# Attention passes of a graph kernel: 64 of 231 edge groups as one-hot matmuls on TensorE, the rest gathered

## The chip, the cores and the metric

One NeuronCore of one Trainium2 chip. The time is the device time of one execution of the whole program, in microseconds; the median of three runs before the change is 11624.68 us (11606.98 to 11636.15).

## What is computed

A graph of 6250 nodes with 64 features and 206250 edges, sorted by destination, goes through eight message-passing layers: three SAGE layers, two weighted GIN layers and three GAT (attention) layers, with residual additions and layer norms between and at the end. The change is about the attention layers, and about the first SAGE pass, which prepares lists for later ones. An attention layer, with 8 heads of 8 features:

```python
h = (x @ W.T).reshape(N, H, C)
alpha_s = jnp.einsum('nhc,hc->nh', h, a_src)
alpha_d = jnp.einsum('nhc,hc->nh', h, a_dst)
e = _leaky_relu(alpha_s[src] + alpha_d[dst])
e_max = jax.ops.segment_max(e, dst, num_segments=N)
e_exp = jnp.exp(e - e_max[dst])
denom = jax.ops.segment_sum(e_exp, dst, num_segments=N)
alpha = e_exp / denom[dst]
msg = alpha[:, :, None] * h[src]
out = jax.ops.segment_sum(msg, dst, num_segments=N)
```

## The kernel before

**Groups.** The edges stand in 231 groups (NG) of 7 x 128 (G columns on P partitions). As they are sorted, the destinations of a group lie in a window of WIN = 32 nodes. Sums and maxima of the destinations are kept transposed in SBUF, features on partitions and nodes along the row: accT (72 rows: 64 sums and 8 denominators), xT (running maxima of the source scores, rows 0 to 7), auxT (rows 0 to 7: alpha of the destination).

**An attention pass** (gat_pass, three times) has five engines in order, each with a body(n) that works on several groups at different stages; the loops are unrolled. GpSimd gathers for each group 7 x 128 rows of 72 numbers from gat_table in DRAM by seven indirect DMAs (L2285), into a ring of GR = 12 buffers. ScalarE (L2380 to L2410) does in body n: factors(n-3), weights(n-5), over_lowest(n), which is the source score minus the lowest (L2399). VectorE in body n: exponents(n-4), shifts(n-2), columns_in_quads(n-3), over_layers(n-1), chosen(n), in_layers(n), turned_choice(n), messages(n-5), add_sums(n-7). TensorE: sums(n-6), values(n-3), shifts(n-2), turn_maxima(n-1), layer_maxima(n). The maximum over the edges of a destination is found by laying the scores in ten layers (LAYERS), so that edges of one destination are in different ones, multiplying with the one-hot of the destination, and a maximum over layers. If a new group raises a destination's maximum, the sums so far are multiplied by a factor. The semaphores that matter below: VectorE's exponents(g) waits for p_ready of weights(g-1) (its buffer z is single); TensorE's values(g) waits for avm_ready of VectorE's columns_in_quads(g), which needs TensorE's shifts(g) of a body earlier; TensorE's layer_maxima(n) waits for VectorE's in_layers(n). SyncE loads each group's destinations.

```python
for n in range(NG + 6):
    body(n)
```

**Cells.** The sage and gin passes don't gather most of their rows. Four groups (GB) make a block, 46 blocks in all, and the edges of a block are scattered by GpSimd (scatter, L1001) into 52 cells (TS), by the source modulo 52, in up to SL = 112 slots. Source s is row s // 52 of cell s % 52 of the node table, which lies in SBUF as X[partition, cell, feature], so that a one-hot of the source's partition (near) times the cell's nodes, split in three bf16 parts, gives the rows (fetch, L1049), and a one-hot of the destination (far_hot, fp32) times the messages gives the sums (add_cells, L1069). A block is worked in 13 pieces (NPC) of 4 cells (PC). The first sage pass makes these lists: slots come from a rank, the number of earlier edges in the same cell (rank_event on TensorE, L1109; earlier_in_bins, place on VectorE), over all 28 columns of the block at once. It stores the near one-hots (near_keep, SyncE, near_table) for all blocks, and for blocks with even number the product of both one-hots (adjacency L1059, keep L1385) and for odd ones the destination and weight of each slot (note, L1393). A check (overflow) sends all passes to a general way where a cell is too full.

The attention pass needs a score and a maximum for each edge, and before the change uses no cells.

## Time and profile before

| | |
|---|---|
| median of 3 runs | 11624.68 us |
| profiled execution | 11634.58 us, span 11632.5 us |
| TensorE busy | 8371.0 us (72%), mean granted clock 0.677 of 2.4 GHz |
| VectorE busy | 7236.0 us (62%) |
| ScalarE busy | 2833.5 us (24%) |
| GpSimd busy | 8097.8 us (70%) |
| DMA | 1285.98 MB, mean 111 GB/s |

Engines: PE is TensorE (PEld its weight loads), DVE VectorE, ACT ScalarE, POOL GpSimd, SP SyncE. The first sage pass runs to about 2430 us, two further sage passes to about 3800, two gin passes to about 4950, and the attention passes from 5140 to the end at 11632.

The page cuts the span in 40 slices and gives busy tenths, the granted clock in tenths of 2.4 GHz, and DMA:

```profile
PE   4878888889999799956666667566666666666665
PEld 3777777768778687835555555455555545555553
DVE  5777777779999654565555556555555565555556
ACT  2444333434444455520000001100000020000001
POOL 5777777737577475727777775677777757777774
PEclk9898888979999898955555555555555555555555
```

A fp32 matmul shows as two MATMUL and two LDWEIGHTS instructions. Shapes read partitions x elements; for TensorE rows x columns of the weights and then of the moving operand.

### The profile page before, as it was taken

The numbers are of one execution on the slowest core, as the hardware profiler recorded it, in microseconds if no ns is written. First come the engines' busy times: TensorE is split into PE (matmuls) and PEld (weight loads), VectorE is DVE, ScalarE is ACT, GpSimd is POOL, SyncE is SP. The second block draws the span as 40 slices with busy tenths as digits, with TensorE's granted clock in tenths as the row PEclk, the third lists the DMA queues.
The fourth block names the chain that finished last, engine by engine and source line by source line (L and its number), as shares of the span: only waits on it lengthen the run. The fifth ranks groups of instructions, "written<-read, shape, count | busy, mean of one in ns | idle before, by whom it ended". The sixth has DMA issues, their size and how long they took to land. (4 is left out here: it accounts for less than half of the span.)

```text
span 11632.5 us, 269882 instructions
## 1 busy us (share of the span) xinstructions
PE 8371.0 (72%) x95122; PEld 6886.6 (59%) x95123; DVE 7236.0 (62%) x21427; ACT 2833.5 (24%) x9590; POOL 8097.8 (70%) x8039
## 2 busy tenths in 40 slices
PE   4878888889999799956666667566666666666665
PEld 3777777768778687835555555455555545555553
DVE  5777777779999654565555556555555565555556
ACT  2444333434444455520000001100000020000001
POOL 5777777737577475727777775677777757777774
PEclk9898888979999898955555555555555555555555
DMA  4666666649899686812222221222222212222221
GB/s 133 189 188 190 188 178 182 187 127 258 222 257 258 193 267 210 254 25 43 43 43 43 43 43 33 43 43 43 43 43 43 43 33 43 43 43 43 43 43 28
DMA packets 1192998, 1285.98 MB, mean 111 GB/s; under 512 B 234298, under 2 KB 1039893, under 8 KB 1191410
## 3 DMA queue, kind: packets, MB, share of 16 engines
q1 hardware_dynamic: 629602, 628.36, 17.7%
q0 software_dynamic: 254464, 283.59, 12.8%
q10 hardware_dynamic: 307600, 356.66, 10.6%
q8 instruction: 788, 12.91, 0.5%
q14 instruction: 544, 4.46, 0.1%
HBM read 982.93 MB, written 284.81 MB: 109 GB/s over the span
## 5 line engine op out<-in xcount | busy, mean ns | idle before, releaser
L2285 POOL DMA_INDIRECT rows<-gat_table,wgt x2457 | 2353.5, 958 | 962.2 <-issue 747.9
L2285 POOL DMA_INDIRECT Y<-gat_table,wgt x2394 | 2293.6, 958 | 729.6 <-issue 729.6
L2466 DVE TENSOR_TENSOR rep<-rep,layers 128x560 f32<-128x560 f32 x693 | 514.9, 743 | 2372.6 <-ACT rep L2399 2372.6
L1001 POOL DMA_INDIRECT bins<-scratch,slots x1288 | 1373.2, 1066 | 500.0 <-issue 384.9
L2311 PE MATMUL bank<-rep,work 128*32 128x80 f32 x11088 | 527.7, 341 | 1495.5 <-DVE rep L2466 1495.5
L2311 PEld LDWEIGHTS bank<-rep,work 128*32 128x32 f32 x11088 | 324.0, 158 | 1836.6 <-DVE rep L2466 1836.6
L2358 PE MATMUL bank<-work,msg 128*72 128x32 f32 x9702 | 1308.7, 309 | 0.0
L2358 PEld LDWEIGHTS bank<-work,msg 128*72 128x72 f32 x9702 | 1215.8, 237 | 44.5
L1191 DVE TENSOR_TENSOR xT<-counts,xT 112x480 f32<-112x480 f32 x1716 | 1114.5, 650 | 80.0 <-issue 48.3
L1069 PE MATMUL bank<-xT 112*64 112x120 f32 (+1 forms) x13728 | 1138.5, 277 | 26.4 <-ACT xT L1379 24.4
L2345 PE MATMUL bank<-scratch,work 128*128 128x64 f32 x2772 | 754.8, 426 | 515.5 <-DVE scratch L2436 515.5
L1012 POOL DMA_INDIRECT rows<-node_table,listed x826 | 916.6, 1110 | 266.1 <-issue 251.0
L1069 PEld LDWEIGHTS bank<-xT 112*64 112x64 f32 (+1 forms) x13728 | 1025.3, 142 | 87.8 <-ACT xT L1379 46.4
L1379 ACT ACTIVATE xT<-xT 112x256 f32<-112x256 f32 x1716 | 712.0, 415 | 1433.7 <-DVE xT L1196 1228.0
L2345 PEld LDWEIGHTS bank<-scratch,work 128*128 128x128 f32 x2772 | 643.5, 323 | 609.5 <-DVE scratch L2436 609.5
L1196 DVE TENSOR_TENSOR xT<-scores,xT 112x256 f32<-112x256 f32 x1344 | 562.7, 419 | 476.0 <-PE scores L1049 431.5
L1569 POOL DMA_INDIRECT rows<-node_table,listed x658 | 698.6, 1062 | 202.0 <-issue 200.1
L2399 ACT ACTIVATE rep<-rows,rep 128x56 f32<-128x56 f32 x351 | 119.8, 341 | 2812.4 <-DMA rows<-gat_table,wgt 2812.4
L2399 ACT ACTIVATE rep<-Y,rep 128x56 f32<-128x56 f32 x342 | 116.7, 341 | 2722.3 <-DMA Y<-gat_table,wgt 2722.3
L1049 PE MATMUL scores<-work 128*128 128x64 bf16 x11344 | 648.5, 195 | 47.8 <-DMA work<-near_table 35.9
L1654 DVE TENSOR_TENSOR scratch<-counts,scratch 112x480 f32<-112x480 f32 x598 | 393.8, 659 | 402.1 <-PE scores L1605 394.3
L1049 PEld LDWEIGHTS scores<-work 128*128 128x128 bf16 x11344 | 525.8, 99 | 87.1 <-DMA work<-near_table 45.4
(277 smaller groups left out, 16940.1 us busy)
## 6 DMA issues: line engine op xcount, KB each, us to landing
xT<-bins ACTq DMA_DIRECT2D x1716, 119.0 KB
work<-adj SPq DMA_DIRECT2D x184, 780.0 KB
work<-near_table SPq DMA_DIRECT2D x1118, 128.0 KB
near_table<-work SPq DMA_DIRECT2D x598, 128.0 KB
xT<-near_table SPq DMA_DIRECT2D x598, 128.0 KB
adj<-work ACTq DMA_DIRECT2D x299, 240.0 KB
bins<-zeros ACTq DMA_DIRECT2D x46, 1547.0 KB, 9.6
work<-in_attr SPq DMA_DIRECT2D x231, 224.0 KB
```

The costliest lines, as they stand in the source:

```text
L1001: nc.gpsimd.indirect_dma_start(bins, bass.IndirectOffsetOnAxis(slots[b % RANK_LEAD][:, r * G + j:r * G + j + 1], 0), binf[r][:, j, :], Non ...
L1012: nc.gpsimd.indirect_dma_start(rows[s][:, k, 0:D], None, table, bass.IndirectOffsetOnAxis(listed_of(n + g0, k), 0)).then_inc(s_rows[s].han ...
L1049: last = nc.tensor.matmul(joint[k % JR][0:SLW, c * D:(c + 1) * D], found[:, c * SLW:(c + 1) * SLW], part_of[:, i * PC + c, :], start=n == ...
L1069: last = nc.tensor.matmul(half_sums(u, c % HALVES), cellf[k % RR][0:SL, c, 0:width], far_hot[k % RR][0:SL, c * MW:(c + 1) * MW], start=i = ...
L1191: nc.vector.tensor_tensor(far_hot[s][0:SL, :].rearrange("p (c m) -> p c m", m=MW), bc(counts[0:SL, 1:MW + 1], [SL, PC, MW], 1), bc(payf[s] ...
L1196: nc.vector.tensor_tensor(cellf[s][0:SL, :, 0:D], joint[k % JR][0:SL, 0:PC * D].rearrange("p (c d) -> p c d", d=D), payf[s][0:SL, :, 0:D], ...
L1379: nc.scalar.activation(cellf[s][0:SL, :, 0:D], cellf[s][0:SL, :, 0:D], ACT.Relu).then_inc(q["cells_ready"].handle, 1)
L1569: nc.gpsimd.indirect_dma_start(rows[s][:, k, 0:D], None, table, bass.IndirectOffsetOnAxis(listed_of(n + g0, k), 0)).then_inc(s_rows[s].han ...
L2285: nc.gpsimd.indirect_dma_start(rows[g % GR][:, j, :], None, gat_table, bass.IndirectOffsetOnAxis(edge_sources[:, g * G + j:g * G + j + 1], ...
L2311: last = nc.tensor.matmul(dense[c * WIN:(c + 1) * WIN, k // QUAD * LH:(k // QUAD + 1) * LH], sels[g % SR][:, j, :], layered[:, j * LH:(j + ...
L2345: last = nc.tensor.matmul(edge[:, h * QUAD * 2 * H:(h * QUAD + n) * 2 * H], choice[g % RR][0:n * WIN, h * P:(h + 1) * P], avm4[0:n * WIN, ...
L2358: last = nc.tensor.matmul(wide[g % 2][0:ROW, 0:WIN], msg[g % R][:, j, :], sels[g % SR][:, j, :], start=j == 0, stop=j == G - 1)
```

## The change

In each attention pass, the four groups of 16 odd-numbered blocks (1, 3, ..., 31), 64 groups, are not gathered. They are worked as blocks of cells; the other 167 groups go as before, over a list `order`.

- The first sage pass stores two more tables for these 16 blocks: far_table, the fp32 one-hots of the destination (far_keep, on SyncE), and far_turned, their transposes in bf16. These are made on TensorE (turn_far: the destination numbers spread over the partitions, in the bank of adjacency) and on ScalarE (keep_turned: the square of the difference, then relu(1 - square), two ACTIVATEs and a store per piece).
- The rank now counts group by group, so that within a cell the edges are in order of destination. That takes 70 matmuls instead of 28 for each block (rank_event).
- A new block `repeats` reads the notes of the 16 blocks and compares slots 8 apart (CELL_LAYERS); if any two have the same destination, all passes go the general way.
- alpha of the destination moves from auxT to accT rows 96 to 103 (ALPHA), and auxT holds gat_table in three bf16 parts, which each pass makes at its start from 13 chunks (table_load, table_high, table_rest, table_middle, table_low). In shifts the copy of alpha comes first and is waited for.
- The ring of gathered rows has 8 buffers (GR) instead of 12.
- The cell work of a block is laid out in 35 steps, a new block every 19 (LAG), in all 320, over the 174 bodies of a pass; half of a body's steps stand before TensorE's layer_maxima and VectorE's chosen, the others at the end; on ScalarE they all stand at the end of the body. In steps 0 to 12 a piece is fetched (cell_fetch), taken by ScalarE (cell_take) and laid in eight layers, and one step later multiplied with the destination one-hots (cell_layer), then reduced (cell_reduce). Step 14 turns the maxima (cell_turn), 15 does the shifts of 120 destinations (cell_shift, cell_column), 16 and 17 carry the destinations' values to the slots by the turned one-hots (cell_value), 17 and 18 the exponents and weights, 18 to 30 the messages, 19 to 31 the sums (cell_sum), 32 to 34 the output is turned and added.

Both one-hots and tables are loaded by SyncE, in rings of 6 (near and turned, 131 KB each) and 4 (far, 215 KB each).

```diff
-GR = 12
+GR = 8
+CELL_LAYERS = 8
+CELL_BLOCKS = 16
+LAG = 19
+LAST = 35
...
-                        for j in range(GT):
-                            last = nc.tensor.matmul(rank_sum, earlier16[:], hot[:, j, :], start=j == 0, stop=j == GT - 1)
+                        for r in range(GB):
+                            of_group = rank_sum[:, r * TS:(r + 1) * TS]
+                            for j in range((r + 1) * G):
+                                last = nc.tensor.matmul(of_group, (earlier16 if j >= r * G else ones16)[:], hot[:, j, :],
+                                                        start=j == 0, stop=j == (r + 1) * G - 1)
...
+                    def keep_turned(b, i):
...
+                        nc.scalar.activation(apart_of, adj_sum[:, 0:PC * SL], ACT.Square, bias=minus_part1[:]).then_inc(q["far_apart"].handle, 1)
...
+            order = [g for g in range(NG) if not (g < GB * NBK and g // GB % 2 == 1 and g // GB // 2 < CELL_BLOCKS)]
+            GN, DELAY = len(order), 7
+            bodies = GN + DELAY
...
+            all_steps = LAG * (CELL_BLOCKS - 1) + LAST
...
+            MAXED, COLUMNS, VALUES, WEIGHED, SUMMED, OUT = NPC + 1, NPC + 2, NPC + 3, NPC + 5, NPC + 6, 2 * NPC + 6
+
+            def active(s):
+
+                return [(k, s - LAG * k) for k in range(CELL_BLOCKS) if 0 <= s - LAG * k < LAST]
+
+            def steps_of(n):
+
+                at = [(n + i) * all_steps // (bodies - 2) for i in [-1, 0]]
+                steps = list(range(max(at[0], 0), min(max(at[1], 0), all_steps)))
+                return steps[:(len(steps) + 1) // 2], steps[(len(steps) + 1) // 2:]
...
+                    def cell_fetch(k, i):
+                        hots = hot_of("near", k, i)
+                        wait(pe, (q["cells_ready"], piece(k, i)), (q["low_ready"], NCH))
+                        for c in range(PC):
+                            for n, part_of in enumerate(table_parts):
+                                last = nc.tensor.matmul(found_bank[0:SLW, c * ROW:(c + 1) * ROW], hots[:, c * SLW:(c + 1) * SLW], part_of[:, i * PC + c, :],
+                                                        start=n == 0, stop=n == 2)
+                        last.then_inc(q["fetched"].handle, 1)
+
+                    def cell_layer(k, i):
+                        fars = far_of("layer", k, i)
+                        wait(pe, (q["cells_ready"], piece(k, i) + 1), (q["layers_reduced"], piece(k, i)))
+                        for c in range(PC):
+                            last = nc.tensor.matmul(layer_bank[0:MW, c * CL:(c + 1) * CL], fars[:, c * MW:(c + 1) * MW], cell_layered[piece(k, i) % 2][0:SL, c * CL:(c + 1) * CL],
+                                                    start=True, stop=True)
+                        last.then_inc(q["cells_layered"].handle, 1)
...
+                    def cell_value(k, h):
+                        wait(pe, (q["column_parts_ready"], k + 1), (q["cell_z_ready"], 2 * k + h))
...
+                    def cell_sum(k, i):
...
+                        for c in range(PC):
+                            last = nc.tensor.matmul(cell_sums[0:MW, 0:ROW], fars[:, c * MW:(c + 1) * MW], cell_msg[piece(k, i) % 2][0:SL, c, :],
+                                                    start=i == 0 and c == 0, stop=i == NPC - 1 and c == PC - 1)
...
                     def body(n):
                         if real(n - 6):
                             sums(n - 6)
...
                         if real(n - 1):
                             turn_maxima(n - 1)
+                        for s in steps_of(n)[0]:
+                            cell_step(s)
                         if real(n):
                             layer_maxima(n)
+                        for s in steps_of(n)[1]:
+                            cell_step(s)
...
+                    def cell_take(k, i):
+                        x = piece(k, i)
+                        wait(ac, (q["fetched"], x + 1), (q["cell_msg_ready"], x - NPC + 1), (q["cells_layered"], x - 1))
+                        found_of = found_bank[0:SL, 0:PC * ROW].rearrange("p (c w) -> p c w", w=ROW)
+                        layers_of = cell_layered[x % 2][0:SL, :].rearrange("p (c l h) -> p c l h", l=CELL_LAYERS, h=H)
+                        nc.scalar.activation(cell_rows[0:SL, i * PC:(i + 1) * PC, :], found_of[:, :, 0:D], ACT.Copy)
+                        nc.scalar.activation(cell_above[0:SL, i * PC:(i + 1) * PC, :], found_of[:, :, D:ROW], ACT.Identity, bias=minus_lowest[0:SL, :])
+                        for n in range(CELL_LAYERS):
+                            last = nc.scalar.activation(layers_of[:, :, n, :], found_of[:, :, D:ROW], ACT.Identity,
+                                                        bias=lowest_layers[0:SL, n:n + 1], scale=cell_layers[0:SL, n:n + 1])
+                        last.then_inc(q["cells_ready"].handle, 1)
...
                         if real(n):
                             over_lowest(n)
-
-                    for n in range(NG + 5):
+                        for s in [*steps_of(n)[0], *steps_of(n)[1]]:
+                            cell_step(s)
+
+                    for n in range(bodies):
                         body(n)
...
+                    def cell_reduce(k, i):
+                        wait(ve, (q["cells_layered"], piece(k, i) + 1))
+                        nc.vector.tensor_reduce(cell_maxima[0:MW, i * H:(i + 1) * H], layer_bank[0:MW, 0:PC * CL].rearrange("p (x h) -> p h x", h=H), AX, ALU.max
+                                                ).then_inc(q["layers_reduced"].handle, 1)
...
                         if real(n - 1):
                             over_layers(n - 1)
+                        for s in steps_of(n)[0]:
+                            cell_step(s)
                         if real(n):
                             chosen(n)
                             in_layers(n)
...
                         if real(n - DELAY):
                             add_sums(n - DELAY)
+                        for s in steps_of(n)[1]:
+                            cell_step(s)
```

## Rows read from the trace of the kernel before

**Rows 1.** Windows: us, busy (x instructions) PE PEld DVE ACT POOL, clock, DMA share, GB/s.

```profile
500.00:1500.00 1000.00, 811.76 (x9910) 732.22 (x9908) 749.64 (x1519) 403.93 (x1243) 781.99 (x716) 0.89 0.65 190
5250.00:6750.00 1500.00, 944.55 (x7139) 762.20 (x7138) 780.10 (x3227) 144.56 (x680) 1137.62 (x1190) 0.50 0.22 43
```

**Rows 2.** Page, costliest groups: L2285, busy, mean ns | idle before, releasers.

```profile
L2285 POOL DMA_INDIRECT rows<-gat_table,wgt x2457 | 2353.5, 958 | 962.2 <-issue 747.9
L2285 POOL DMA_INDIRECT Y<-gat_table,wgt x2394 | 2293.6, 958 | 729.6 <-issue 729.6
```

**Rows 3.** Lines L2285 and L2521 in the first attention pass: min/median/max ns, first, last.

```profile
L2285 POOL DMA_INDIRECT rows<-gat_table,wgt x819: 940/944/1508, 5139.9 to 7178.4; - x164
...
L2521 DVE TENSOR_TENSOR accT<-accT,bank x231: 182/183/186, 5214.2 to 7205.8; 72x32 f32 x116
```

**Rows 4.** Waits, 5300 to 6900 us: us in total, times, longest.

```profile
ACT rep L2399 <- DMA Y<-gat_table,wgt: 723.2, 91, 8.9
```

**Rows 5.** Groups of GpSimd, 500 to 1500 us, columns as in rows 2.

```profile
L1001 POOL DMA_INDIRECT bins<-scratch,slots x570 | 616.2, 1081 | 173.8 <-issue 173.2 <-ACT scratch L1403 0.6
L1012 POOL DMA_INDIRECT rows<-in_x,listed x146 | 166.8, 1143 | 44.5 <-issue 44.5
```

**Rows 6.** Timeline, second sage pass: start, us, engine, line, operation, idle before it.

```profile
3304.16 0.52 PE L1049 MATMUL scores<-work 128*128 128x64 bf16 x12
...
3304.72 0.42 DVE L1196 TENSOR_TENSOR xT<-scores,xT 112x256 f32<-112x256 f32 x1 [0.16 <-PE scores L1049]
```

**Rows 7.** Timeline, one body of the first attention pass.

```profile
7003.87 0.21 ACT L2384 ACTIVATE Y<-dif 8x32 f32<-8x32 f32 x1
7003.99 0.74 DVE L2466 TENSOR_TENSOR rep<-rep,layers 128x560 f32<-128x560 f32 x1 [3.34 <-ACT rep L2399]
...
7004.25 0.25 ACT L2392 ACTIVATE msg<-zpos 128x56 f32<-128x56 f32 x1
...
7004.79 0.76 PE L2311 MATMUL bank<-rep,work 128*32 128x80 f32 x16 [2.05 <-DVE rep L2466]
...
7005.83 0.21 DVE L2449 TENSOR_TENSOR z<-rows,bank 128x56 f32<-128x56 f32 x1
...
7006.18 0.94 POOL L2285 DMA_INDIRECT Y<-gat_table,wgt  x1 [0.30 <-issue]
...
7007.15 0.18 DVE L2502 TENSOR_TENSOR U<-xT,auxT 8x32 f32 x1 [0.60 <-issue]
...
7008.82 0.30 DVE L2475 TENSOR_REDUCE rep<-bank 128x8 f32<-128x160 f32 x1
7008.94 0.93 PEld L2345 LDWEIGHTS bank<-scratch,work 128*128 128x128 f32 x4 [0.84 <-DVE scratch L2436]
...
7010.91 0.60 PE L2324 MATMUL bank<-ident,rep 128*8 128x128 f32 x2
```

**Rows 8.** Timeline of ScalarE, second gin pass.

```profile
4555.90 1.94 ACT L1583 ACTIVATE scratch<-scores,scratch 112x64 f32<-112x64 f32 x8 [1.52 <-PE scores L1596]
```

**Rows 9.** Groups of ScalarE, 5300 to 6900 us, columns as in rows 2.

```profile
L2390 ACT ACTIVATE zpos<-z 128x56 f32<-128x56 f32 x182 | 42.3, 232 | 0.0
...
L2399 ACT ACTIVATE rep<-rows,rep 128x56 f32<-128x56 f32 x91 | 31.1, 341 | 722.6 <-DMA rows<-gat_table,wgt 722.6
```

**Rows 10.** Windows of 4 us in the first sage pass, columns as in rows 1.

```profile
648.00:652.00 4.00, 2.02 (x27) 1.38 (x25) 3.90 (x8) 2.35 (x7) 3.39 (x3) 1.00 1.03 313
652.00:656.00 4.00, 0.51 (x12) 0.42 (x12) 3.22 (x12) 1.69 (x5) 3.08 (x4) 0.78 0.79 204
...
660.00:664.00 4.00, 4.00 (x54) 3.95 (x54) 2.01 (x4) 1.94 (x6) 3.09 (x4) 0.50 0.47 149
664.00:668.00 4.00, 4.00 (x46) 3.94 (x46) 0.30 (x2) 0.89 (x3) 3.05 (x4) 0.94 0.63 181
```

**Rows 11.** Timeline of TensorE, first sage pass: the ranking's matmuls.

```profile
661.76 1.40 PE L1109 MATMUL bank<-hot,earlier 128*128 128x52 bf16 x28
```

**Rows 12.** Windows, second sage pass, columns as in rows 1.

```profile
2750.00:3000.00 250.00, 236.95 (x4827) 202.07 (x4822) 237.50 (x552) 104.39 (x246) 196.34 (x177) 1.00 0.93 258
```

438 lines of the change are left out of this document (403 added, 35 removed).

## The prediction

> **What bounds the kernel now.** I read the windows first. The span falls into a sage part, a gin part and three attention passes, and most of the change happens in the passes. In a steady stretch of a pass no computing engine is full and TensorE's granted clock is at its lower level, 1.2 GHz [rows 1]. The instructions of the gather show why: the 2457 + 2394 indirect DMAs on GpSimd take 0.958 us each, and the fixed gap before them ("issue", 748 + 730 us in all) another 0.305; nothing else holds them up but the start of a pass [rows 2]. That is 1.263 us for one and 8.84 us for the seven of a group; 231 groups make 2042 us. The first pass has its first gather at 5139.9 and its last accumulation at 7205.8: 2066 us, GpSimd and a short tail [rows 3]. In a stretch of 1600 us ScalarE waits 723 us for the rows of one part of the ring, and the other part has as much [rows 4]. So GpSimd bounds a pass, and the others have slack inside a body. In the first sage pass GpSimd is full too: in 1000 us it is busy 783 us, and the gaps between its 716 instructions take the rest [rows 5].
>
> **What the change takes away.** 64 groups of each pass are no longer gathered: 64 x 8.84 = 566 us of GpSimd per pass, 1697 us for three. If GpSimd stayed the bound, 167 groups would take 1476 us. The question is whether the other three engines, which now carry the cells of those groups, can turn a body in 8.84 us.
>
> **What it adds, counted.** There are 16 blocks of 13 pieces, LAG 19 steps apart, each 35 steps long: 15 x 19 + 35 = 320 steps laid over 174 bodies, nearly two a body. Applying the new steps_of to the bodies gives 83 bodies with two full steps (a piece fetched, laid in layers, and an older block's piece summed), 15 with one, 14 with one full and one light step, 45 with light steps alone (turning maxima, shifts, values), 6 with two steps of the first block, which has no sums beside it, and 11 with sums or next to nothing.
> A full step costs TensorE 12 bf16 matmuls (fetch), then 4 fp32 matmuls for the layers and 4 for the sums; each fp32 matmul is two instructions. Fetch: 12 matmuls of 64 columns span 0.52 us at 2.4 GHz [rows 6]; with 72 columns I take 0.55, and 0.9 at 1.2 GHz. fp32: the weights decide. Four loads of 128 columns take 0.93 us at 1.2 GHz [rows 7], 0.23 each; I take 0.215 for 120 columns, so 8 instructions take 1.7 us, and 0.85 at 2.4 GHz.
> A full step costs VectorE a reduction of 256 columns (160 take 0.30 us [rows 7], so 0.4) and a product of 112x256 (0.42 [rows 6]).
> A full step costs ScalarE ten ACTIVATEs and a copy, by far its largest load: cell_take. Nearest row: eight of 112x64 from PSUM with a per-partition scale take 1.94 us, 0.24 each [rows 8]. The eight layer copies have a per-partition scale and a per-partition bias. What one such operand adds is seen in two operations on 128x56: without one 0.232 us, with a bias 0.341 us [rows 9], so 0.11 more. I take 0.31 for each of the eight, 2.5 us, plus 0.6 us for the two others: 3.1 us. The lower end is 2.45 us, if the second operand is free.
> The Trainium skill ("ScalarE: Activation LUTs", What ACT_TABLE_LOAD costs) gives 186 ns plus 0.833 ns per element, 93 ns for each pointer operand, and an overlap of 93 ns back to back; by it cell_take is 3.06 us. This trace agrees for one operand (0.232 to 0.341); it has no ACTIVATE with two in a row.
>
> **Where it lies: the step that decides.** Work per engine would still fit. What doesn't is the order. Every engine runs its instructions in order, and a loop closes from body to body. VectorE's exponents(n-4) wait for p_ready, that is, for ScalarE's weights(n-5). Those stand in ScalarE's body n behind all cell steps of body n-1, so behind its second cell_take. That waits for TensorE's second cell_fetch of body n-1, which stands behind layer_maxima, behind the whole first step, and behind values, whose input comes from VectorE's shifts and columns_in_quads, which follow the exponents. A gathered row doesn't enter this loop. Its length in a body with two full steps:
> - exponents to the start of values: 5.83 to 8.94 in the body shown, 3.11 us [rows 7]. The shifts' copy of alpha is now first and waited for: 3.25 us.
> - values, shifts, turned maxima on TensorE: from 8.94, with the turning matmuls started at 10.91 and in the array for some 0.25 more: 2.2 us, half at the higher clock [rows 7].
> - the first step's sum 1.7, fetch 0.9; its cell_take 3.1 us. The second fetch waits for that take (there is one bank of found rows), and by then TensorE's layers, layer_maxima and second sum (0.85 + 0.3 + 0.85) are done at the higher clock. Second fetch 0.55, second take 3.1.
> - factors and weights: from 3.87 to 4.50, 0.63 us [rows 7]; hand-overs, 0.06 us each as between VectorE's 7004.73 and TensorE's 7004.79, seven of them: 0.4 [rows 7].
> Sum: 3.25 + 2.2 + 1.7 + 0.9 + 3.1 + 0.55 + 3.1 + 0.63 + 0.4 = 15.8 us. With TensorE at 2.4 GHz throughout: 3.25 + 1.1 + 0.85 + 0.55 + 3.1 + 0.55 + 3.1 + 0.63 + 0.4 = 13.5. At 1.2 GHz throughout TensorE's own path is longer than the first take, and the sum is 3.25 + 2.2 + 1.7 + 0.9 + 1.7 + 0.5 + 1.7 + 0.9 + 3.1 + 0.63 + 0.4 = 17.0.
> **Which clock.** In the first sage pass the clock falls from 2.4 to 1.2 GHz after TensorE was busy 2.02 and then 0.51 us in stretches of 4 us, is at 1.2 in a later one with 4.00 us busy, and is back in the one after [rows 10]. In a body with two full steps TensorE has about 6 us without work, while ScalarE takes the second piece and VectorE does exponents and shifts, and then 7 to 8 us nearly without a gap. So I expect it to fall in that gap and rise inside the body: four bodies in five as in the first sum, one as in the second, 15.4 us.
> The Trainium skill ("TensorE: Matmul & The Clock Gate", Part 1) says that low clock is the default and sustained activity lifts it; by that rule alone, with more TensorE work, one would take 2.4 GHz, and a pass would be 83 x 1.9 = 158 us shorter. The stretches above show that the gap counts as well.
> **The other bodies.** With one full step the second fetch and take drop out: 3.25 + 2.2 + 1.7 + 0.9 + 3.1 + 0.63 + 0.3 = 12.1 us. Mixed ones: 12.5. Two steps of the first block: 15.8 less the sum, 14.1. Light ones hold lumps: 84 and then 72 bf16 matmuls with 16 columns (28 with 52 columns take 1.40 us [rows 11], so 4.2 and 3.6 us; nothing narrower is in the trace, bounds 2.4 and 4.5), VectorE's column shift (seven chained operations of about 0.25 us, and 0.6 us of issue [rows 7]), three operations on 112x224 and back. Between 9 and 13; I take 11. The last eleven: 9.
> A pass: 83 x 15.4 + 15 x 12.1 + 14 x 12.5 + 45 x 11 + 6 x 14.1 + 11 x 9 = 1278 + 182 + 175 + 495 + 85 + 99 = 2314 us, and 15 us more at its start, where the table is split into three bf16 parts before the first body. That is 2329 against 2066 now: 263 us longer, 789 for three.
> **What else it touches.** The ring of gathered rows shrinks from 12 groups to 8: nothing, as GpSimd now waits for its consumers. Loads: 208 + 208 one-hots of 131 KB and 416 of 215 KB, 144 MB a pass, some 62 GB/s, beside the 43 GB/s and 0.22 share of now [rows 1]; the engines moved 258 GB/s in the second sage pass [rows 12], so they are hidden, each being issued a body ahead by SyncE. Lower end nothing, upper end 2 us per lump, 64 us a pass.
> First pass: 72 MB more to store, on ScalarE's and SyncE's queues, in its first two thirds. GpSimd stays the bound, but its indirect DMAs grow with the traffic: the scatter takes 1.081 us at a DMA share of 0.65 where the gather of a pass takes 0.94 at 0.22 [rows 1, 5, 7]; 0.05 us more on 35 x 31 instructions is 55 us. The ranking's 42 extra matmuls per block, 2.1 us by the 1.40 us for 28 [rows 11], and the turned one-hots lie in TensorE's and ScalarE's slack (busy 812 and 404 of 1000 us [rows 5]); if that cover is gone, 46 x 2.1 = 97 us. The repeats block: 15 us. I take 70 us, from 10 to 170.
>
> **The sum.** Profiled execution 11634.6 us (span 11632.5) + 789 + 70 = 12494; the median of the runs is 10 us below the profiled one, so 12480 us in round figures.
>
> **Rivals.**
> 1. The pass stays GpSimd's (the loop overlaps in a way that I don't see): 11635 - 3 x (566 - 15) + 70 = 10052 us. For it: work per engine. A body of now has 5.5 us of TensorE, 4.6 of VectorE and 0.85 of ScalarE [rows 1]; times 167, plus 208 full steps of 4.3, 0.82 and 3.3 us, plus 125 or less for the lumps, that is 1940 us for TensorE at 1.2 GHz, not much over half of it at 2.4, and 1060 and 860 for the others. Against it: the order of waits above, which leaves no body with two full steps under 12 us. Chance 0.05.
> 2. The loop is there but short: clock at 2.4 GHz throughout and the eight layer copies at 0.24 us. A full body is 13.5 - 1.3 = 12.2, one-step bodies 9.8, light ones 10, the rest a tenth less: 83 x 12.2 + 15 x 9.8 + 14 x 11 + 45 x 10 + 6 x 12 + 90 = 1926 + 15. That is 125 us less than now, times three, + 70: 11320 us. This is the faster side's main case. It decides below an average body of 11.7 us ((2066 - 15 - 23) / 174, the 23 being a third of the 70). For it: TensorE in the second sage pass, at 2.4 GHz for 250 us with gaps of its own [rows 12]. Chance 0.18.
> 3. The loop is longer: 1.2 GHz throughout (17.0), light bodies 13 with waits for the one-hots, first pass 170: a pass is 83 x 17.0 + 182 + 185 + 45 x 13 + 90 + 99 + 15 = 2567, 501 more; 11635 + 1503 + 170 = 13308 us. For it: TensorE's 1.2 GHz everywhere in the passes now. Against: the rise inside a busy stretch [rows 10]. Chance 0.15.
> 4. The new check finds a destination twice in a layer, and all runs go the general way: no row has its price, only that it is slower. Destinations are sorted within a cell by the new ranking, so nine equal in one cell of some 69 would be needed. Chance 0.01.
> My forecast: 0.61, from 11600 to 13000.
> Faster by over 0.3% (about what a measurement of this kernel can tell from no change): rivals 1 and 2, 0.23, and the forecast's lowest end 0.02, in all 0.25; within 0.3%: 0.03; slower: 0.72. The range, 11400 to 13050, leaves out rival 1, a part of 2 and most of 3.
>
> **What would show it.** Right: GpSimd's gather no longer has only "issue" before it but waits, for VectorE's messages; the wait of ScalarE's above for DMA is gone; ScalarE's cell_take comes right behind TensorE's fetch, and VectorE's exponents behind ScalarE's weights; a pass of about 2330 us, bodies in two kinds, some 15 and 11 us; a granted clock between 0.5 and 1; cell_take about 3.1 us. Wrong: GpSimd without waits, or full bodies of 12 us. The prediction fails most easily on the clock in a full body and on the price of the layer copies.

## The result and the profile after

| | median us | range | runs |
|---|---|---|---|
| before | 11623.92 | 11606.98 to 11636.15 | 4 |
| changed | 12917.78 | 12915.27 to 12941.45 | 4 |

The ratio is 1.1119, 95% interval 1.1100 to 1.1138: the change makes the kernel 11.2% slower. The profiled execution has a span of 12917.0 us, 1284.5 more than the one of before.

Where do the 1284.5 us lie? Three landmarks answer that, each the first or last start of one line: the scatters of the first sage pass (GpSimd), the gathers of the attention passes (GpSimd), and the accumulations of a pass (VectorE). The scatters of the two kernels, columns as in rows 3 (before, then changed):

```profile
L1001 POOL DMA_INDIRECT bins<-scratch,slots x1288: 952/958/2442, 100.2 to 2341.8; - x184
```

```profile
L1081 POOL DMA_INDIRECT bins<-scratch,slots x1288: 952/958/2435, 101.9 to 2728.1; - x184
```

Then the gathers at the start of the first attention pass of the changed kernel, against [rows 3]:

```profile
L2531 POOL DMA_INDIRECT rows<-gat_table,wgt x84: 939/944/1252, 5547.4 to 5686.4; - x84
```

- First sage pass: the last scatter starts 386 us later, and the first attention gather 407.5 us later (5547.4 against 5139.9).
- Attention passes: first accumulation to last takes 2261.7, 2259.9 and 2259.5 us, where it took 1991.6, 1995.6 and 1993.5: 800 us more for three. The line of the first pass, against [rows 3]:

```profile
L2911 DVE TENSOR_TENSOR accT<-accT,bank x167: 182/183/186, 5646.9 to 7908.6; 72x32 f32 x167
```

- Each pass also has 25 to 26 us more between its first gather and its first accumulation, or between its predecessor's last accumulation and its own first: 77 us.
- 407.5 + 800 + 77 = 1284.5. Two thirds of the loss are in the passes, one third ahead of them.

In the passes the profile looks like this. Windows of the changed kernel, columns as in rows 1:

```profile
500.00:1500.00 1000.00, 742.30 (x8992) 662.18 (x8991) 600.19 (x1210) 450.89 (x1199) 594.34 (x567) 0.81 0.63 186
5800.00:7500.00 1700.00, 1384.63 (x11361) 1236.92 (x11361) 745.95 (x2847) 540.18 (x2243) 810.51 (x848) 0.50 0.35 91
```

GpSimd fell from 76% busy [rows 1] to 48%, and TensorE rose from 63% to 81%. No engine is full, the granted clock is 0.50 (1.2 GHz), and yet a pass is longer. The page's line of the gather, against [rows 2], and the waits of 5800 to 7500 us (engine, line, releaser: us in total, times, longest) say what GpSimd does instead:

```profile
L2531 POOL DMA_INDIRECT rows<-gat_table,wgt x2646 | 2524.9, 954 | 2884.9 <-DVE msg L2878 1963.0
```

```profile
ACT work L2741 <- PE scores L2623: 821.9, 152, 9.0
DVE z L2839 <- ACT msg L2719: 512.1, 96, 7.2
POOL rows L2531 <- DVE msg L2878: 496.2, 82, 8.7
PEld bank L2591 <- DVE scratch L2826: 274.4, 100, 4.8
PE bank L2591 <- DVE scratch L2826: 260.8, 97, 4.7
```

Read from top to bottom these are one loop. ScalarE waits for the fetch, VectorE for ScalarE's weights, TensorE for VectorE's shifts, and GpSimd, outside it, for a buffer that VectorE gives back. One body in the timeline:

```profile
6501.10 0.38 ACT L2741 ACTIVATE work<-scores 112x256 f32<-112x256 f32 x1 [8.20 <-PE scores L2623]
...
6501.55 2.26 ACT L2744 ACTIVATE work<-scores,lowest_layers,cell_layers 112x32 f32<-112x32 f32 x8
...
6505.00 0.93 PE L2623 MATMUL scores<-auxT,scratch 128*128 128x72 bf16 x12
...
6505.97 0.38 ACT L2741 ACTIVATE work<-scores 112x256 f32<-112x256 f32 x1 [2.04 <-PE scores L2623]
...
6506.42 2.26 ACT L2744 ACTIVATE work<-scores,lowest_layers,cell_layers 112x32 f32<-112x32 f32 x8
...
6508.89 0.25 ACT L2719 ACTIVATE msg<-zpos 128x56 f32<-128x56 f32 x1
...
6509.23 0.21 DVE L2839 TENSOR_TENSOR z<-rows,bank 128x56 f32<-128x56 f32 x1 [6.06 <-ACT msg L2719]
...
6512.84 1.09 PE L2591 MATMUL bank<-scratch,work 128*128 128x64 f32 x4 [3.07 <-DVE scratch L2826]
...
6515.43 0.94 POOL L2531 DMA_INDIRECT rows<-gat_table,wgt  x1 [8.11 <-DVE msg L2878]
...
6517.97 0.38 ACT L2741 ACTIVATE work<-scores 112x256 f32<-112x256 f32 x1 [8.60 <-PE scores L2623]
```

From one take of a first piece to the next (6501.10 to 6517.97) 16.9 us pass, about one body; each engine in turn has a gap in it, TensorE's longest 3.07 us.

### The profile page after: what moved, and what is told of

Same layout as the page of the kernel before. It is cut to its first block and busy times, and to the rows that moved or that the text cites. A ratio compares the mean times of both kernels' runs of the same rounds, so it can differ in the third digit from the quotient of the medians.

```text
span 12917.0 us, 319100 instructions
## 1 busy us (share of the span) xinstructions
PE 10369.9 (80%) x115263; PEld 9002.7 (70%) x115264; DVE 7167.7 (55%) x20083; ACT 4741.4 (37%) x16468; POOL 6758.9 (52%) x6695
## 5 line engine op out<-in xcount | busy, mean ns | idle before, releaser
L2741 ACT ACTIVATE work<-scores 112x256 f32<-112x256 f32 x624 | 239.0, 383 | 3280.9 <-PE scores L2623 3264.4
L2744 ACT ACTIVATE work<-scores,lowest_layers,cell_layers 112x32 f32<-112x32 f32 x4992 | 1410.3, 404 | 0.0
L2591 PE MATMUL bank<-scratch,work 128*128 128x64 f32 x2004 | 543.7, 425 | 1052.2 <-DVE scratch L2826 1051.8
L2531 POOL DMA_INDIRECT Y<-gat_table,wgt x861 | 827.7, 961 | 875.8 <-DVE msg L2878 645.0
L2659 PEld LDWEIGHTS scores<-scratch,Y 112*120 112x120 f32 x4992 | 1045.6, 315 | 199.1 <-issue 199.0
L2659 PE MATMUL scores<-scratch,Y 112*120 112x72 f32 x4992 | 1167.8, 416 | 0.0
L2631 PE MATMUL scores<-work,Y 112*120 112x64 f32 x4992 | 1149.7, 412 | 10.6 <-ACT work L2744 10.6
L2631 PEld LDWEIGHTS scores<-work,Y 112*120 112x120 f32 x4992 | 1066.0, 319 | 27.6 <-issue 27.6
L2839 DVE TENSOR_TENSOR z<-rows,bank 128x56 f32<-128x56 f32 x378 | 80.3, 212 | 1574.1 <-ACT msg L2719 1522.6
L2604 PE MATMUL bank<-work,msg 128*72 128x32 f32 x7014 | 946.2, 309 | 0.0
L2604 PEld LDWEIGHTS bank<-work,msg 128*72 128x72 f32 x7014 | 879.0, 237 | 32.1
```

The costliest lines, as they stand in the source:

```text
L2531: nc.gpsimd.indirect_dma_start(rows[g % GR][:, j, :], None, gat_table, bass.IndirectOffsetOnAxis(edge_sources[:, order[g] * G + j:order[g] ...
L2591: last = nc.tensor.matmul(edge[:, h * QUAD * 2 * H:(h * QUAD + n) * 2 * H], choice[g % RR][0:n * WIN, h * P:(h + 1) * P], avm4[0:n * WIN, ...
L2604: last = nc.tensor.matmul(wide[g % 2][0:ROW, 0:WIN], msg[g % R][:, j, :], sels[g % SR][:, j, :], start=j == 0, stop=j == G - 1)
L2631: last = nc.tensor.matmul(layer_bank[0:MW, c * CL:(c + 1) * CL], fars[:, c * MW:(c + 1) * MW], cell_layered[piece(k, i) % 2][0:SL, c * CL: ...
L2659: last = nc.tensor.matmul(cell_sums[0:MW, 0:ROW], fars[:, c * MW:(c + 1) * MW], cell_msg[piece(k, i) % 2][0:SL, c, :], start=i == 0 and c ...
L2744: last = nc.scalar.activation(layers_of[:, :, n, :], found_of[:, :, D:ROW], ACT.Identity, bias=lowest_layers[0:SL, n:n + 1], scale=cell_la ...
```

## The experiments

Every time is beside runs of the kernel before on the same chip (medians 11616 to 11627). For the passes the question was first whether the loop sets a body or something else does, and then what keeps the clock at its lower level; for the first sage pass, which of the new pieces of work costs the time.

### The first pass alone

All 231 groups are gathered again in the attention passes; the stores of the first sage pass, the ranking, the ring of 8 and the table's parts stay.

```
-            order = [g for g in range(NG) if not (... g // GB // 2 < CELL_BLOCKS)]
+            order = list(range(NG))
...
-            all_steps = LAG * (CELL_BLOCKS - 1) + LAST
+            all_steps = 0
```

> The changed kernel with the attention passes gathering all 231 groups again and doing no cell steps; the first sage pass (new tables, new ranking, check for repeats), the table split and the ring of 8 stay. It splits the 1294 us between the first pass and the three attention passes. Theory (loop through ScalarE in the passes, 3 x about 320 us, and about 330 us in the first pass by the two profiles): about 11970 us. Rival (the ring of 8 buffers, the table split or the moved alpha cost time in the passes by themselves): more than 12050 us.

Measured: 12070.85 us (12067.29 to 12074.42), ratio 1.0391 (1.0370 to 1.0411). That is some 100 us above what the theory gave and in the range of the rival, but not for the rival's reason. Its passes take 2005.2, 1999.5 and 1999.6 us from first to last accumulation, so the smaller ring and the moved alpha together cost 14, 4 and 6 us, and the stretches between passes are some 2 us longer. The first accumulation comes at 5626.7 against 5214.2. The work ahead of the passes costs about 412 us, not 70. The cells cost the rest, 12918 - 12071 = 847 us, some 282 a pass.

### The layer copies

ScalarE's eight layer copies of a piece become one ACTIVATE that writes zeros: the layer masks are left out of the computation.

```
-                        for n in range(CELL_LAYERS):
-                            last = nc.scalar.activation(layers_of[:, :, n, :], ..., ACT.Identity, bias=..., scale=...)
+                        last = nc.scalar.activation(layers_of, bc(found_of[:, :, D:ROW], ...), ACT.Copy, scale=0.0)
```

> The changed kernel with the eight layer copies of cell_take replaced by one ACTIVATE of 112x256 that writes zeros, so that the layers' masks and with them the maxima of the cells are left out; every other instruction stays. ScalarE's cell_take falls from 2.7 to about 0.9 us. Theory (the loop runs through ScalarE's second take): a body with two full steps falls from 16.6 to about 14.8 us, one with one full step from 11.7 to 9.9, the first block's from 13.7 to 10.1: 230 us a pass, 12230 us in all. Rival (ScalarE's work hides, TensorE or the loads decide): within 30 us of 12918.

Measured: 12286.49 us, ratio 1.0576 (1.0555 to 1.0597): 631 us less than the changed kernel, 210 a pass. That is the theory's case, with 12230 expected. ScalarE's busy time was never the limit (540 of 1700 us), and halving it gives a tenth of the pass back, because one of the two takes of a full body lies in the loop. cell_take fell from 2.71 to 0.84 us, 1.9 us less, and so did a full body, from 16.55 to 14.66 us in the mean of the first pass. Had both takes been in the loop, it would have lost twice as much. The two takes of a body start 4.87 us apart with the layer copies (6501.10 and 6505.97 above) and without them:

```profile
6499.77 0.38 ACT L2741 ACTIVATE work<-scores 112x256 f32<-112x256 f32 x1 [8.54 <-PE scores L2623]
...
6504.64 0.38 ACT L2741 ACTIVATE work<-scores 112x256 f32<-112x256 f32 x1 [3.91 <-PE scores L2623]
```

Between them it is TensorE's own work that counts, as in the prediction's sum for 1.2 GHz throughout. The clock stayed at 0.50 with TensorE busy 1254 of 1400 us (6100 to 7500).

### ScalarE's cell steps one body later

The computation is whole. ScalarE does the cell steps of body n - 1 in body n, behind the weights, so the weights no longer wait for the second take.

```
-                        for s in [*steps_of(n)[0], *steps_of(n)[1]]:
+                        for s in [*steps_of(n - 1)[0], *steps_of(n - 1)[1]]:
                             cell_step(s)
...
-                    for n in range(bodies):
+                    for n in range(bodies + 1):
                         body(n)
```

> The changed kernel with ScalarE's cell steps one body later: in body n it does the steps of body n-1, behind weights and over_lowest of body n. Same work, other order. Theory (what costs is that weights stand behind the body's second cell_take): the take leaves the loop, and a body with two full steps is bound by TensorE's own work at 1.2 GHz, 2.2 + 0.5 + 2.2 for the group and 2 x 4.2 for the steps, about 13.2 us instead of 16.6; one-step bodies 9.3 instead of 11.7: about 320 us a pass, 11960 us in all, less if TensorE, now nearly without gaps, is granted 2.4 GHz. Rival (the loads or another chain decide): above 12700 us.

Measured: 11844.50 us (11834.11 to 11860.83), ratio 1.0200 (1.0183 to 1.0217), 1073 us less than the changed kernel by a move of one line. Passes: 1915.9, 1911.9 and 1915.0 us, so 80 us shorter than before the change. Of the 83 full bodies of the first pass the one in the middle took 16.59 and now takes 13.59 us; 52 of them lie within 0.05 us of that, and the mean is 13.12. The theory had 13.2 and 11960 us. Window of this kernel:

```profile
6100.00:7500.00 1400.00, 1327.74 (x11086) 1196.90 (x11078) 730.31 (x2792) 523.71 (x2159) 795.56 (x814) 0.50 0.41 106
```

TensorE is busy 95% now and sets the full body. This confirms the loop, and it takes the gap out of the argument on the clock: I had expected the clock to be kept low by TensorE's gap of some 3 us a body. The gap is gone and the clock is still 0.50. There is no measurement of the changed kernel with that gap filled and nothing else moved.

### What raises the clock

To this kernel 8 bf16 matmuls are added ahead of each fetch, into the bank that the fetch then writes over. They compute nothing that is used.

```
+                        for c in range(8):
+                            nc.tensor.matmul(found_bank[0:SLW, 0:PC * ROW], hots[:, 0:SLW], hots[:, 0:PC * ROW], start=True, stop=True)
                         for c in range(PC):
```

> The kernel with ScalarE's cell steps one body later (11844.5 us; full bodies of 13.59 us, TensorE 95% busy, clock 0.50), and ahead of each piece's 12 fetch matmuls 8 more bf16 matmuls of 288 columns into the same bank, which the fetch then writes over: the computation is unchanged. 16 of them in a full body; at 288 columns 1.2 GHz gives an estimated 0.24 us each, 3.84 us a body. Theory C, the clock stays low because so little of TensorE's busy time moves columns (weights of 120 and 128 columns for 32 to 72 moving ones): the granted clock rises to 1.00 in the full bodies, TensorE's part is halved (17.4 to about 9 us), and a body is set by ScalarE at 11 to 13.5 us: whole time 11500 to 11850 us in spite of the added work. Theory D, wide matmuls among them change nothing: clock 0.50, full bodies of 17.4 us, about 400 us a pass more, whole time 12900 to 13050 us. A rise in some bodies alone gives times between.

Measured: 11463.58 us (one run). More work, and 381 us less: theory C's direction, a little below its range, and in a part of the bodies only. Windows of this kernel, the first in a stretch of full bodies at one level, the second at the other:

```profile
6165.00:6170.00 5.00, 5.00 (x56) 4.42 (x55) 4.54 (x17) 3.50 (x15) 3.90 (x4) 1.00 0.52 140
6170.00:6175.00 5.00, 4.46 (x60) 3.93 (x59) 1.62 (x6) 2.76 (x11) 3.77 (x4) 1.00 0.61 167
```

```profile
6070.00:6075.00 5.00, 5.00 (x40) 4.67 (x37) 2.39 (x6) 3.50 (x15) 0.00 (x0) 0.50 0.25 77
```

Of the 83 full bodies of the first pass 36 run at 1.00 from end to end and take 10.18 us in the middle; 14 run at 0.50 from end to end: seven of them take 17.43, and the other seven, each the first behind light bodies, about 8.2, as in the kernel without the added matmuls. Over 5800 to 7100 us the clock is 0.70. The busy share says nothing about the level: 4.46 of 5 us busy at 1.00, 5.00 of 5 at 0.50. So the busy time of the kernel without them (95%) was not what was missing; these matmuls were. What in them the clock answers to the runs don't show: no kernel with as many narrow ones, or as many in fp32, was run.

### Which part of the first pass costs 386 us

The waits of the changed kernel in 500 to 1500 us have a line that was almost empty before: GpSimd's scatter waiting for ScalarE's pack.

```profile
POOL bins L1081 <- ACT scratch L1514: 250.6, 60, 8.3
PEld bank L1217 <- DMA work<-in_attr: 134.3, 41, 5.8
PE bank L1217 <- DMA work<-in_attr: 124.5, 36, 5.7
```

Before, the first was 0.6 us in all. The timeline of one such wait, from the bottom up: the scatter waits for the pack, the pack for TensorE, TensorE 5.60 us for a load of attributes, and SyncE issued that load at 740.01, right behind far_keep (L1024), which had waited for the destination one-hots that VectorE finished at 739.63.

```profile
738.98 0.65 DVE L1285 TENSOR_TENSOR xT<-counts,xT 112x480 f32<-112x480 f32 x1
739.65 0.32 SPq L1024 DMA_DIRECT2D far_table<-xT  x1
740.01 0.50 SPq L996 DMA_DIRECT2D work<-in_attr  x1
...
741.77 1.57 PEld L1217 LDWEIGHTS bank<-scratch,work 128*64 128x64 f32 x14 [5.60 <-DMA work<-in_attr]
...
746.89 0.22 ACT L1514 ACTIVATE scratch<-scratch 128x28 f32<-128x28 f32 x1
...
747.38 0.96 POOL L1081 DMA_INDIRECT bins<-scratch,slots  x1 [8.30 <-ACT scratch L1514]
```

The rival is the turned one-hots, whose two ACTIVATEs stand ahead of the pack. Two kernels leave one of the two out, both on top of the one that gathers all groups. (The trace has 208 transfers of either kind, not the 224 that the texts below give, and the turned one-hots are those of the destination.) The first drops the calls of far_keep:

```
-                                if turned_too(b):
-                                    far_keep(b, u, it, i)
```

> Like the run that gathers all 231 groups in the passes (12070.85 us), and the first pass does not store the destination one-hots (far_keep, 224 transfers of SyncE, is left out of the program; nothing in this kernel reads them). In the changed kernel the last scatter of the first pass starts at 2728.1 us, before at 2341.8: 386 us of the 433 us by which its attention passes start later. In a block of cells that is kept, TensorE waits 5 to 8 us in front of an attribute matmul for a load that SyncE has issued 2 us earlier, right behind far_keep, which had waited for the destination one-hots of the same piece. Theory A, SyncE's order: with far_keep gone the loads run ahead again; last scatter at about 2400 us (2340 to 2480), whole time about 11740 us (11680 to 11830). Theory B, the turned one-hots (two ACTIVATEs of 0.63 and 0.67 us a piece on ScalarE ahead of the pack, and TensorE's four matmuls that wait for them): last scatter stays at 2650 to 2730, whole time 11990 to 12075 us.

Measured: 11785.82 us (ratio 1.0138, 1.0118 to 1.0159), last scatter at 2452.5:

```profile
L1079 POOL DMA_INDIRECT bins<-scratch,slots x1288: 952/958/2664, 103.2 to 2452.5; - x184
```

The other drops turn_far and keep_turned:

```
-                                elif turned_too(earlier_piece[0]):
-                                    turn_far(*earlier_piece)
...
-                            if i > 1 and turned_too(b):
-                                keep_turned(b, i - 2)
```

> Like the run that gathers all 231 groups in the passes (12070.85 us), and the first pass does not turn, copy and store the source one-hots (turn_far and keep_turned are left out: 4 matmuls, two ACTIVATEs and a transfer of ScalarE's queue for each of 224 pieces; nothing in this kernel reads them); far_keep stays. Theory A, SyncE's order: far_keep still stands ahead of the attribute loads, so most of the loss stays: last scatter of the first pass at 2580 to 2730 us, whole time 11920 to 12075 us. Theory B, the turned one-hots: last scatter at about 2400 us, whole time about 11740 us. If both this run and the one without far_keep gain half, the two share one cycle: DVE's one-hot comes later because ScalarE and TensorE are late, and the load waits for it.

Measured: 12025.18 us (ratio 1.0344, 1.0323 to 1.0365), last scatter at 2670.9. The kernel that both are built on has its last scatter at 2738.0, 396 us later than before the change. So leaving far_keep out gives 286 us of them back, and leaving the turned one-hots out 67. It is far_keep, as theory A has it; whether its place or its traffic costs, this pair can't tell, and the kernels below can. The rest, some 40 us if the two simply add, is left for the ranking, which was not tried alone. The repeats come behind the last scatter: they and what else lies there make the 21 us between the 386 and the 407.5.

### far_keep behind the loads

The whole computation, with ScalarE's steps one body later, and far_keep at the end of the piece.

```
-                                if turned_too(b):
-                                    far_keep(b, u, it, i)
...
                                 for n in due_at(b + 1, i):
                                     plain_loads(n)
+                            if first_pass and turned_too(b):
+                                far_keep(b, u, it, i)
```

> The whole computation. ScalarE's cell steps one body later (11844.5 us), and in the first pass SyncE issues far_keep behind the attribute loads of its piece instead of ahead of them. Theory A, SyncE's order: the loads no longer wait for the destination one-hots; last scatter of the first pass at 2400 us (2340 to 2520) instead of 2728, whole time about 11530 us (11470 to 11640), which would be at or below the kernel before (11616). Theory B, the turned one-hots: no change, 11820 to 11860 us.

Measured: 11672.78 us (11663.28 to 11679.32), ratio 1.0040 (1.0026 to 1.0054), last scatter at 2563.5. The direction is A's, the size is half: 172 us. As I read it, far_keep now waits behind the load of its own piece and holds up the next piece's; the kernel with far_keep two pieces later, below, bears that out.

### Together, and two sizes

All four kernels here have ScalarE's steps one body later. The first adds the 8 matmuls to the kernel above.

> The whole computation: ScalarE's cell steps one body later, 8 more matmuls of 288 columns ahead of each piece's fetch (11463.6 us together, full bodies of 10.17 us where the clock is 1.00 and 17.4 us where it is 0.50), and far_keep behind the attribute loads of its piece (11844.5 to 11672.8 us without the added matmuls). If the two edits touch different stages and add up: 11463.6 - 171.7 = 11292 us, 11250 to 11340. Rival: the clock in the passes rises by chance and the passes are not steady from run to run, then anything from 11200 to 11600 us, with intervals far wider than the 0.1% of the others.

Measured: 11283.63 us (11236.62 to 11342.66), ratio 0.9698 (0.9674 to 0.9723). The two edits add up (11292 expected). The runs spread over 0.9%, where kernels with a steady 0.50 in the passes spread over 0.1 to 0.3%. In this trace bodies of 10.2 us and of 17.4 us take turns, and a few more of one kind would be enough to move the time so far.

Then 14 instead of 8 added matmuls a piece (range(14) in the loop above):

> As the one before, with 14 added matmuls instead of 8 ahead of each piece's fetch. TensorE's part of a full body is 8.7 us at clock 1.00 with 8 of them and some 10.2 us with 14 (12 more a body, 0.12 to 0.14 us each); at clock 0.50 it is 17.4 and some 20.3 us. If the clock now stays at 1.00 through nearly all full bodies, these take about 10.3 us and the whole time is 11050 to 11250 us; if the share of full bodies at 1.00 stays about half, the added work costs 1.5 us a body and the whole time is 11350 to 11500 us.

Measured: 11556.42 us (ratio 0.9947, 0.9927 to 0.9967), 273 us more, which neither case allowed. The clock is higher (0.79 over 5800 to 7000 us against 0.68 over 5800 to 7100), but no more full bodies of the first pass are at 1.00 from end to end (28 of 83, against 31 with 8), and these take 11.64 us in the middle, 1.5 us more than 10.17. In 48 others the clock changes within the body, mostly in drops of 3 to 7 us, and many of them take 13.3. As I read it, the added matmuls stand ahead of the fetch, the fetch is in the path of the pieces, and 12 more of them a body cost there what they take; the clock that I counted on to pay for it did not come in whole bodies. No further run tests this.

Next, 8 a piece and 8 for each gathered group, ahead of layer_maxima, into the bank that it writes over:

```
+                        for k in range(8):
+                            nc.tensor.matmul(dense[:, 0:P], ones16[:], earlier16[:], start=True, stop=True)
                         for k in range(2 * QUAD):
```

> As the first of this call (8 added matmuls a piece), and 8 bf16 matmuls of 128 columns more ahead of each gathered group's layer matmuls, in the bank that these write over. In the trace with the 8 a piece alone the clock is back at 0.50 after the light bodies, in which TensorE has gaps of 2 us and no added work. If the light bodies are where the clock is lost, it now stays at 1.00 in most of the pass: 11050 to 11230 us. If they are not, the work costs 0.5 to 0.9 us a body: 11300 to 11450 us.

Measured: 10908.97 us (10893.30 to 10924.63), ratio 0.9389 (0.9369 to 0.9410). Passes take 1664, 1667 and 1658 us; the clock over 5800 to 7100 us is 0.79. Of the 83 full bodies of the first pass 53 are now at 1.00 from end to end (31 with the 8 a piece alone), at 10.18 us in the middle. The clock falls still in light bodies and comes back in full ones, mostly 27 to 41 us later. The time is below both ranges. Most of the gain lies in the full bodies (11.0 us in the mean of the first pass, against 12.7 with the 8 a piece alone); why work in the gathered groups does that is not shown.

Last, far_keep two pieces later than its piece, so that its wait is over when SyncE comes to it:

```
+                            if first_pass and i > 1 and turned_too(b):
+                                far_keep(b, u, it, i - 2)
+                            elif first_pass and i < 2 and b and turned_too(b - 1):
+                                far_keep(*after(b, u, it, -1), NPC + i - 2)
```

> As the first of this call, with far_keep two pieces later, behind the loads, so that its wait for the destination one-hots is over when SyncE comes to it. Last scatter of the first pass: 2728 us in the changed kernel, 2563.5 with far_keep behind the loads of its own piece, 2452.5 without it. If it is the wait that costs, the last scatter comes at 2440 to 2490 us and the whole time is 70 to 110 us below the first run of this call; if it is the transfers themselves (112x480 f32 each, 224 of them, on a queue and on engines that are 0.6 busy), it stays at 2530 to 2570 us and so does the time.

Measured: 11136.17 us (11107.61 to 11164.73), ratio 0.9585 (0.9553 to 0.9617), last scatter at 2436.2, so 110 us earlier than with far_keep behind its own piece (2545.9) and no later than with far_keep left out (2452.5):

```profile
L1083 POOL DMA_INDIRECT bins<-scratch,slots x1288: 952/958/2438, 101.4 to 2436.2; - x184
```

The 208 transfers cost nothing that the last scatter shows; it was their wait. The other 38 of the 147 us are within what such kernels differ by from run to run.

### Everything that helped

> The whole computation, with everything that helped: ScalarE's cell steps one body later, 8 added matmuls a piece, far_keep two pieces later, and 16 added matmuls a gathered group instead of 8. The run with 8 a group took 10909.0 us with far_keep behind its own piece; far_keep two pieces later took 147 us off the kernel without them. If both add up and 16 a group does what 8 did: 10909.0 - 147.4 = 10762 us. In the trace with 8 a group the clock falls to 0.50 in the light bodies still and comes back some 20 us later; if 16 a group shortens that, 10620 to 10740 us. If the fall has another cause, the added work costs 0.4 to 0.9 us in each of 522 bodies and the time is 10800 to 11200 us.

Measured: 10765.43 us (10751.46 to 10770.74), ratio 0.9267 (0.9251 to 0.9282): 7.3% faster than before the change, 16.7% faster than the changed kernel, with the same computation. The sum of the parts, 10762, holds; 16 added matmuls a group in place of 8 gave little or nothing of their own (the three passes are 33 us shorter in all, 0.3% of the kernel). Its scatters, the accumulations of its first pass and its window:

```profile
L1083 POOL DMA_INDIRECT bins<-scratch,slots x1288: 952/958/2437, 101.3 to 2428.5; - x184
```

```profile
L2917 DVE TENSOR_TENSOR accT<-accT,bank x167: 182/183/186, 5338.2 to 6977.9; 72x32 f32 x167
```

```profile
5800.00:7100.00 1300.00, 1213.98 (x13904) 1038.05 (x13902) 811.53 (x2806) 561.43 (x2169) 805.61 (x816) 0.80 0.44 115
```

Its passes take 1639.7, 1670.0 and 1645.9 us, against 1991.6 to 1995.6 before the change, with GpSimd busy 62%.

## Why the prediction was right or wrong

**The direction and its reason: right.** I said that the order of waits, not the work per engine, would set a body, and named the loop. The waits show it link by link, and taking one link out gave 1073 us. The timeline's gap in front of GpSimd and the end of ScalarE's wait for DMA are as I wrote. The sum for 1.2 GHz throughout holds in its parts too: from the first take to the second it has 1.7 + 0.5 + 1.7 + 0.9 = 4.8 us, and the trace 4.87.

**The lengths of the bodies: right by their own terms.** From the starts of VectorE's exponents (L2839) in the first pass:

| bodies | number | predicted us | measured us |
|---|---|---|---|
| two full steps | 83 | 15.4 (17.0 at 1.2 GHz throughout) | 16.55 |
| one full step | 15 | 12.1 | 11.72 |
| full and light | 14 | 12.5 | 12.67 and 11.90 |
| light | 37 and 7 | 11 | 11.31 and 7.05 |
| two of the first block | 4 | 14.1 | 13.75 |

**The copies: slightly too dear.** cell_take lasts from 6501.10 to 6503.81, 2.71 us, not 3.1. The eight layer copies take 2.26 us, not 2.5.

**The clock: the step that failed in the passes.** Under "Which clock" I wrote that it would fall in a gap of about 6 us and rise inside each full body. TensorE's longest gap in the body shown is 3.07 us, and the clock never rose in a pass: 0.50 in every window. 83 bodies at 16.55 instead of 15.4 are 95 us a pass. Everything else in a pass was shorter than I put it, by 66 us in sum, which leaves the 29 us a pass by which I was low: the table accounts for some 25 of the 66, and most of what is left lies at the two ends of a pass, in eight bodies that the table doesn't have. So a miss upward and one downward partly cancel. I had read [rows 10] as a matter of gaps, and two runs say that gaps alone don't decide: 95% busy with full bodies without a gap stays at 0.50, and the same kernel with added matmuls is at 1.00 in many bodies. Full rows of busy time from one stage are no forecast of the level in another with other matmuls. The Trainium skill ("TensorE: Matmul & The Clock Gate", Part 1), by which the level follows how busy the array has been, is no better a forecast here than my gap was, if busy is read as the profile's busy share (95% at a clock of 0.50). That also refutes what I said for rival 2, that TensorE's 2.4 GHz in the second sage pass [rows 12] speaks for 2.4 GHz here.

**The start of a pass.** I put the table split at 15 us. The 25 to 26 us by which the landmarks at the start of a pass lie further apart can't be set against it, since they hold the first bodies with cells as well; where all groups are gathered and nothing waits for the split table, they are 2 us. What the split costs in the changed kernel is not measured alone.

**The first pass: the term that was mis-sized.** 70 us predicted, upper bound 170; measured 407.5 to the first gather, 386 of them in the first sage pass. I priced far_keep as traffic and the turned one-hots as slack. What it cost was its place: a transfer that waits for VectorE, ahead of a load that TensorE needs, on a queue that goes in order. I had written "on ScalarE's and SyncE's queues" and did not ask who stands behind. The upper bound of 97 us, ranking without cover, was a bound of another term. (It was worked out from [rows 11]; the busy times of 812 and 404 us beside it stand in [rows 1], not in [rows 5].)

**The sum.** 263 us a pass predicted, 292 measured ((1284.5 - 407.5) / 3), and 70 against 407.5. The forecast of 12480 is 438 us low, 338 of them by what lies ahead of the passes, 88 by the passes, and the rest by rounding 12494 down. That 12918 lies in the range all the same owes as much to the width of the range as to the terms: it is near the upper end of 13050, and a third of the loss came out of a term whose own upper bound, 170, it passed by far.

**The rivals.** Rival 1 (GpSimd stays the bound) and rival 2 (a short loop) are refuted for this kernel. Rival 3 is right on the clock and wrong on the light bodies. Rival 4, the general way, did not occur, since the passes have the bodies that were counted. What rival 2 saw was there to be had, though: with the loop cut and the clock up a pass takes some 1650 us, and 11320 was not even low.

**Still open.** What in the added matmuls raises the clock. Whether the kernel before would gain from added matmuls: it wasn't run, and its passes waited for GpSimd (7 x 1.263 us a group), which they would not shorten. Whether the 40 us left ahead of the last scatter are the ranking's. Why 14 added matmuls a piece cost more than 8.

## What to carry to other kernels

Before putting work on an engine with slack, follow its in-order list once round: if a product that the next iteration needs comes out behind the new work, the new work's whole latency is added, whatever the busy share is. On a DMA queue the same holds for a store that waits: put it behind the loads, late enough that its wait is over when its turn comes. And where TensorE sits at the lower clock although it is nearly full, try added matmuls that nothing uses before counting the stage as bound by TensorE; one profile tells. Try few: here 8 a piece took 381 us off, and 14 in their place cost 273.

## What the runs showed of the hardware

- TensorE can be busy 1327.74 of 1400 us at a granted clock of 0.50. With 16 more bf16 matmuls of 288 columns in each full body it reached 1.00 in 36 of 83 full bodies from end to end, and these went from 13.59 to 10.18 us in spite of them.
- Where the level varied most inside the passes (0.68 over 5800 to 7100 us), the runs of one kernel spread over 0.9%; where it was 0.50 throughout, over 0.1 to 0.3%, and over 0.2% in the last kernel, where it was 0.80.
- An ACTIVATE of 112x32 from PSUM with both a per-partition scale and a per-partition bias lasts 0.402 us in the middle (below), but eight in a row last 2.26 us, so they start 0.27 us apart. The Trainium skill ("ScalarE: Activation LUTs", What ACT_TABLE_LOAD costs) gives 186 + 27 + 2 x 93 = 399 ns for one by its figures, with which this row agrees; its overlap of 93 ns would give, as an estimate from that page, 0.31 us apart and 2.54 us for eight, which is more than the 0.27 and 2.26 us measured.

```profile
L2744 ACT ACTIVATE work<-scores,lowest_layers,cell_layers x1227: 380/402/430, 5799.8 to 7500.0; 112x32 f32<-112x32 f32 x176
```
